# Self attention: the causal mask moves into stack rows and small column tiles, and the maxima's parts move from VectorE to GpSimd

## The reference

```python
# x: (16, 128, 256) float32; H = 16 heads of HD = 16
qkv = x @ Wqkv.T + bqkv
q, k, v = (to_heads(z) for z in jnp.split(qkv, 3, axis=-1))
q, k = _rope(q), _rope(k)
att = jnp.einsum('bhqd,bhkd->bhqk', q, k) * scale
att = jnp.where(jnp.tril(jnp.ones((t, t), dtype=bool)), att, -jnp.inf)
att = jax.nn.softmax(att, axis=-1)
y = jnp.einsum('bhqk,bhkd->bhqd', att, v)
y = y.transpose(0, 2, 1, 3).reshape(b, t, c) @ Wo.T + bo
...
x = _layernorm(x + y, axis=-1)
```

## Time and profile before

| | |
|---|---|
| median of 3 runs | 1186.73 us (1185.58 to 1187.6) |
| profiled execution | 1184.21 us |
| its span | 1182.4 us |
| granted clock, mean | 0.987 |
| PE busy over the span | 1113.7 us (94%) |
| DVE, ACT, Pool busy | 954.8, 669.1, 661.2 us |

### The profile page before, as it was taken

One profiled execution on the slowest core, in us unless ns is written; L12 is line 12 of the kernel. 1 busy time (PEld: TensorE's weight loads), 2 busy tenths in 40 slices (PEclk: granted clock), 3 DMA queues, 4 the chain that ended last, 5 costly groups with the idle time before them and its releaser, 6 DMA issues.

```text
span 1182.4 us, 30629 instructions
## 1 busy us (share of the span) xinstructions
PE 1113.7 (94%) x11732; PEld 920.0 (78%) x11732; DVE 954.8 (81%) x2219; ACT 669.1 (57%) x1703; POOL 661.2 (56%) x714
## 2 busy tenths in 40 slices
PE   6899999799999999888999999999999999999997
PEld 5667666566666766556899899999999899988887
DVE  6768877887878878867788888888888888868977
ACT  5466564577777777564555444444444444558663
POOL 4467564645555555264778554444544455737665
PEclk9899999999999999989999999999999999999999
DMA  5875544354444444302111000000000100101111
GB/s 160 212 185 132 128 125 112 97 138 123 126 121 131 119 126 126 104 21 89 61 66 55 1 1 1 1 1 1 1 1 1 37 2 1 37 19 36 37 37 36
DMA packets 107491, 83.05 MB, mean 70 GB/s; under 512 B 74172, under 2 KB 95804, under 8 KB 107346
## 3 DMA queue, kind: packets, MB, share of 16 engines
q1 hardware_dynamic: 107345, 81.10, 24.6%
HBM read 57.02 MB, written 23.07 MB: 68 GB/s over the span
## 4 chain that ended last, share of the span: by engine, by line
PE 56%; DVE 14%; issue 6%; POOL 4%; ACT 2%; SPq 1%; DMA 0%; POOLq 0%; DVEq 0%; ACTq 0%
PE bank L1632 5%; PE bank L1633 5%; PE bank L1634 5%; PE bank L1688 4%; PE bank L1661 4%; PE bank L663 4%; PE bank L641 3%; PE bank L560 3%; DVE B_nr L803 2%; PE bank L1648 2%; PE bank L1703 2%; PE bank L1701 2%; PE bank L1702 2%; PE bank L1649 2%; PE bank L1650 2%
## 5 line engine op out<-in xcount | busy, mean ns | idle before, releaser
L1936 POOL TENSOR_TENSOR C_QK<-C_t1b,C_t2b 128x512 f32<-128x512 f32 x128 | 168.8, 1319 | 227.2 <-DVE C_t2b L1775 226.6
L1772 DVE SCALAR_TENSOR_TENSOR C_t1b<-bank,C_bcol,C_tabs 64x512 f32<-64x512 f32 x256 | 192.0, 750 | 38.4 <-PE bank L1634 34.3
L803 DVE TENSOR_REDUCE B_nr<-bank 128x4 f32<-128x512 f32 x256 | 164.3, 684 | 24.3 <-PE bank L602 23.8
L1062 ACT ACTIVATE PT<-bank 128x512 f32<-128x512 f32 x224 | 130.1, 596 | 92.4 <-PE bank L641 90.8
L1632 PE MATMUL bank<-C_XTh,C_Wh 128*128 128x512 f32 x256 | 112.4, 439 | 5.7 <-DVE C_XTl L1621 1.9
L1868 ACT ACTIVATE C_P<-bank,C_nm 128x128 f32<-128x128 f32 x256 | 90.7, 367 | 34.2 <-DVE C_nm L1785 32.6
L1887 ACT ACTIVATE C_V<-bank 128x512 f32<-128x512 f32 x64 | 38.1, 597 | 124.1 <-PE bank L1650 122.5
L1633 PE MATMUL bank<-C_XTl,C_Wh 128*128 128x512 f32 x256 | 101.7, 397 | 0.0
L1634 PE MATMUL bank<-C_XTh,C_Wl 128*128 128x512 f32 x256 | 101.2, 395 | 0.0
L663 PE MATMUL bank<-PT,vpool 128*32 128x128 f32 x2048 | 97.1, 285 | 2.0 <-ACT OTf L1072 2.0
L1775 DVE SCALAR_TENSOR_TENSOR C_t2b<-bank,C_bcol,C_tabs 128x512 f32<-128x512 f32 x128 | 96.1, 751 | 1.8
(11 more groups left out here) (271 smaller groups left out, 3495.8 us busy)
## 6 DMA issues: line engine op xcount, KB each, us to landing
Adrq<-PB SPq DMA_DIRECT2D x16, 192.0 KB, 3.0
Adrk<-PB SPq DMA_DIRECT2D x16, 192.0 KB, 3.2
stk<-Adrq SPq DMA_DIRECT2D x16, 192.0 KB
stk<-Adrk SPq DMA_DIRECT2D x16, 192.0 KB
Bdrq<-PB SPq DMA_DIRECT2D x16, 192.0 KB, 3.0
stk<-Bdrq SPq DMA_DIRECT2D x32, 96.0 KB
Bdrk<-PB SPq DMA_DIRECT2D x16, 192.0 KB, 2.8
stk<-Bdrk SPq DMA_DIRECT2D x32, 96.0 KB
```

Of the source, the lines that this page charges most:

```text
L803: e.tensor_reduce(dst, bank[n % 2][:, :].rearrange("p (a b) -> p a b", a=4), AX.X, ALU.max, negate=True).then_inc(sem("m_dve"), 1)
L1062: e.activation(pt_of(n)[:, :], bank2(n)[:, :], ACT.Exp).then_inc(sem("e_act"), 1)
L1772: e.scalar_tensor_tensor(out=v4(t1b[kq][lo:lo + 64, :]), in0=v4(o[hi:hi + 64, :]), scalar=bc[hi:hi + 64, :], in1=tabsC[hi:hi + 64, 2 * kq ...
L1936: e.tensor_tensor(QK[v % 3][:, kq, :], t1b[kq][:, :], t2b[kq][:, :], ALU.add).then_inc(sem("rc_pool"), 1)
```

## The change

Three things:

1. The mask matmuls L595 and L632 of self attention go. Blocks of 32x32 above the diagonal get their large negative value through three more stack rows: rows 96 to 98 hold, for each of the first three blocks, which columns are that block (one side) and -1e30 where the block is later (the other side); the rows of maxima and ones move to 99 to 101. So pass1's matmuls have 99 rows instead of 96, pass2's 102 instead of 99. The four blocks on the diagonal are added by a new function `causal_blocks`, four column-tile matmuls of 128 columns for each unit and pass, behind the scores; they give the signals `s_pe` and `t_pe`. In a step below 64 PE's order becomes pass1, pass2, the blocks of pass1's unit, the blocks of pass2's unit, pv. The constant rows come in two DMAs instead of one.
2. `shift_parts` runs on Pool for both attentions, and first in Pool's step.
3. `turned` is four instead of two steps behind the parts for g < 16. ACT's copy and SP's DMA follow, to step 4g + 9.

```diff
@@ turned
-    turned = {shift_step(g) + (2 if g < 17 else 4 if g < 31 else 2): g for g in range(32)}
+    turned = {shift_step(g) + (4 if g < 16 else 2 if g < 17 else 4 if g < 31 else 2): g for g in range(32)}
@@ shift_parts, its callers
-    def shift_parts(e, q, g, name):
+    def shift_parts(e, q, g):
...
-        e.tensor_copy(nmb[L][:, :, :, 0, :], heads(nr)).then_inc(sem(name), 1)
-        q.wait_ge(name, 4 * b + 1)
+        e.tensor_copy(nmb[L][:, :, :, 0, :], heads(nr)).then_inc(sem("sh_pool"), 1)
+        q.wait_ge("sh_pool", 4 * g + 1)
...
@@ dve_ab
-            if s in shifts and shifts[s] < 16:
-                shift_parts(e, q, shifts[s], "sh_dve")
@@ pool_ab
+            if s in shifts:
+                shift_parts(e, q, shifts[s])
             if s in INITS:
                 init_values(*INITS[s])
...
-            if s in shifts and shifts[s] >= 16:
-                shift_parts(e, q, shifts[s], "sh_pool")
@@ pass1
-                if not L:
-                    q.wait_ge("consts", 1)
-                    q.wait_ge("ld_m", 48)
-                    e.matmul(scores, causalTb[:, :], identb[:, :].unsqueeze(1).to_broadcast([128, 4, 128]),
-                             start=True, stop=False, skip_group_check=True)
...
-                    rows, h = (slice(64 * t, 64 * t + 48), hs[j] % 16) if L else (slice(0, 96), hs[j])
+                    rows, h = (slice(64 * t, 64 * t + 48), hs[j] % 16) if L else (slice(0, 99), hs[j])
...
-                    if j == 3:
+                    if L and j == 3:
                         m.then_inc(sem("s_pe"), 1)
@@ pass2
-                if not L:
-                    q.wait_ge("consts", 1)
-                    e.matmul(bank2(n)[:, :].rearrange("p (a b) -> p a b", a=4), identb[:, :],
-                             causalTb[:, :].unsqueeze(1).to_broadcast([128, 4, 128]), start=True, stop=False, skip_group_check=True)
                 q.wait_ge(*shift_sem(b + 16 * L))
...
-                    rows, h = (slice(64 * t, 64 * t + 54), hs[j] % 16) if L else (slice(0, 99), hs[j])
+                    rows, h = (slice(64 * t, 64 * t + 54), hs[j] % 16) if L else (slice(0, 102), hs[j])
...
+        def causal_blocks(o, left, right, name):
+
+            for g in range(4):
+                own = slice(32 * g, 32 * g + 32)
+                m = e.matmul(o[own, :].rearrange("p (a b) -> p a b", a=4)[:, :, own], left[:, own],
+                             right[:, own].unsqueeze(1).to_broadcast([128, 4, 32]), start=False, stop=True, skip_group_check=True)
+            m.then_inc(sem(name), 1)
...
@@ pe_ab, the order in a step
                 if pass2_units(s):
                     pass2(pass2_units(s))
+            for n in pass1_units(s):
+                if n < NA:
+                    causal1(n)
+            for n in pass2_units(s):
+                if n < NA:
+                    causal2(n)
+            if s < NA:
                 for n in pv_units(s):
                     pv(n)
@@ sp_ab
-                row = 64 * hg + 48 if L else 96
+                row = 64 * hg + 48 if L else 99
...
-            load(STK[96:99, :, :].rearrange("p (i s) x -> p i s x", s=32)[:, :, 16:32, :],
-                 ot[0:3, :].rearrange("p (s x) -> p s x", x=128).unsqueeze(1).to_broadcast([3, 10, 16, 128]), "ones_A")
+            for half, rows in enumerate((3, 6)):
+                load(STK[96:96 + rows, :, :].rearrange("p (i s) x -> p i s x", s=32)[:, :, 16 * half:16 * half + 16, :],
+                     edge[3 * half:3 * half + rows, :].rearrange("p (s x) -> p s x", x=128).unsqueeze(1).to_broadcast([rows, 10, 16, 128]),
+                     "ones_A")
```

More of the change, by code:

```diff
@@ L132, in program @@
     tabs_ready = ("ld_A", 32), ("ld_B", 48)
-    ot = I["c_one"]
+    ot, edge = I["c_one"], I["c_edge"]
     NA, NN = 64, 320
@@ L462, in split @@
             e.tensor_tensor(pb[:, 2, :, :], y_[:, :, :], pb[:, 1, :, :], ALU.subtract).then_inc(sem(sp(kp, 0)[0]), 1)
-    def shift_parts(e, q, g, name):
-        L, b = divmod(g, 16)
+    def shift_parts(e, q, g):
+        L = g // 16
         q.wait_ge("m_dve", last_unit(g, NK[L] - 1) + 1)
@@ L471, in shift_parts @@
         heads = lambda a: a[:, :, :].rearrange("p k (g h) -> p g k h", h=16)
-        e.tensor_copy(nmb[L][:, :, :, 0, :], heads(nr)).then_inc(sem(name), 1)
-        q.wait_ge(name, 4 * b + 1)
[L474 to L478, removed]
+        e.tensor_copy(nmb[L][:, :, :, 0, :], heads(nr)).then_inc(sem("sh_pool"), 1)
+        q.wait_ge("sh_pool", 4 * g + 1)
+        e.tensor_tensor(heads(nb[L]), heads(nr), nmb[L][:, :, :, 0, :], ALU.subtract).then_inc(sem("sh_pool"), 1)
+        q.wait_ge("sh_pool", 4 * g + 2)
+        e.tensor_copy(nmb[L][:, :, :, 1, :], heads(nb[L])).then_inc(sem("sh_pool"), 1)
+        q.wait_ge("sh_pool", 4 * g + 3)
+        e.tensor_tensor(nmb[L][:, :, :, 2, :], heads(nb[L]), nmb[L][:, :, :, 1, :], ALU.subtract).then_inc(sem("sh_pool"), 1)
     def pe_ab(e, steps):
@@ L585, in pass1 @@
                     if not L:
-                        q.wait_ge("ones_A", 16)
+                        q.wait_ge("ones_A", 32)
                 if n % U[L] == 0 or (L and n % 8 == 0):
@@ L600, in pass1 @@
                     i3 = b % len(QS[L])
-                    rows, h = (slice(64 * t, 64 * t + 48), hs[j] % 16) if L else (slice(0, 96), hs[j])
+                    rows, h = (slice(64 * t, 64 * t + 48), hs[j] % 16) if L else (slice(0, 99), hs[j])
+                    alone = bool(kd) if L else j == 0
                     m = e.matmul(bank[n % 2][:, j * 128:j * 128 + 128], QS[L][i3][rows, h, :], (AS if kd else KS[L])[i3][rows, h, :],
-                                 start=bool(kd), stop=bool(kd) or j == 3, skip_group_check=not kd)
-                    if j == 3:
+                                 start=alone, stop=bool(kd) or bool(L and j == 3), skip_group_check=not kd)
+                    if L and j == 3:
                         m.then_inc(sem("s_pe"), 1)
@@ L608, in shift @@
             L = g // 16
-            q.wait_ge(*(("sh_pool", 4 * g - 60) if L else ("sh_dve", 4 * g + 4)))
+            q.wait_ge("sh_pool", 4 * g + 4)
             q.wait_ge("consts", 1)
@@ L638, in pass2, with causal1, causal2 @@
                     i3 = b % len(QS[L])
-                    rows, h = (slice(64 * t, 64 * t + 54), hs[j] % 16) if L else (slice(0, 99), hs[j])
+                    rows, h = (slice(64 * t, 64 * t + 54), hs[j] % 16) if L else (slice(0, 102), hs[j])
                     alone = bool(L) and (adds_mask(n) or not is_masked(n))
                     m = e.matmul(bank2(n)[:, j * 128:j * 128 + 128], (AS if kd else KS[L])[i3][rows, h, :], QS[L][i3][rows, h, :],
-                                 start=alone, stop=alone or j == 3, skip_group_check=not alone)
-                    if j == 3:
+                                 start=alone or not (L or j), stop=alone or bool(L and j == 3), skip_group_check=not alone)
+                    if L and j == 3:
                         m.then_inc(sem("t_pe"), 1)
+        def causal_blocks(o, left, right, name):
[4 more added lines that the diff above has]
+            m.then_inc(sem(name), 1)
+        def causal1(n):
+            q.wait_ge("consts", 1)
+            q.wait_ge("ld_m", 48)
+            causal_blocks(bank[n % 2], causalTb, identb, "s_pe")
+        def causal2(n):
+            causal_blocks(bank2(n), identb, causalTb, "t_pe")
         def pv(n):
@@ L800, in maxima @@
             if n % U[L] == 0 and b >= 2:
-                q.wait_ge("sh_pool" if L else "sh_dve", 4 * b - 4)
+                q.wait_ge("sh_pool", 4 * (b + 16 * L) - 4)
             q.wait_ge("s_pe", n + 1)
@@ L2430, in tables @@
     c["c_one"][3:6] = 0
+    block = np.arange(2048) % 128 // 32
+    r = np.arange(3)[:, None]
+    c["c_edge"] = np.concatenate([block == r, np.where(block > r, f(-1e30), f(0)), np.ones((3, 2048))]).astype(f).astype(bf)
     c["c_pick"] = np.repeat(np.eye(32, dtype=f), 3, axis=0).astype(bf)
```

## The result

The changed kernel is slower: 1203.38 us (median of 4 runs, 1198.78 to 1205.31) against 1186.15 for the kernel before, a ratio of 1.0154 (95% interval 1.0131 to 1.0177). The forecast was 1188.3 with a range to 1197. It was the fastest of the four runs; between the medians lie 17.2 us.

The account below looks back on a forecast made before the run. PE was taken to pace self attention (109.86 of 114.00 us busy). On 1184.21, 8.0 − 12.0 − 1.5 = −5.5 at step 54, then + 6.6 − 0.4 + 0.9 = +1.6; from the median 1186.73, 1188.3 us, range 1176 to 1197.

Parts of the forecast that it names:

- +8.0 early: PE ahead of group 0's pass2: DMA behind 12 stack loads, +9.1, −1.9 swallowed, +0.8 low clock; range 7 to 9.
- −13.5 in the middle: Steps 14 to 53: 12.0 us from 0.30 saved in each of 40 PE steps, plus 1.5 from DVE's relief.
- +7.1 late: Groups 12 to 14: DMA behind series of 12 loads, +6.6; old wait gone at step 72, −0.4; low clock, +0.9.
- The second load of constants ... I take nothing.: SP's queue ahead of all its steps: one more issue, 0 to 0.9 us, taken as nothing.
- What leaves a step of PE's moves all later steps forward.: Self attention's full stretch: PE, in order and 96% busy, passes on each step's saving of 0.30 us (0.21 to 0.33).
- the later maxima: DVE's maxima start some 0.3 us later in a step, but are wanted only two steps on: nothing.
- DVE's relief: Parts moved to Pool relieve DVE, whose maxima and copies partly cause PE's 4.1 us idle: 0 to 3, taken 1.5.
- the late queue doesn't hold PE: Rival, groups 12 to 14: SP's DMA comes early enough that PE has no late wait; 1178 us, chance 0.23.
- the early wait is absorbed: Rival, group 0: other PE work that waits behind fills its wait later; gain 7 more, 1181 us, chance 0.05.
- Pool becomes the pace: Rival, self attention: Pool's waits stay beside the added parts, half of the 12.0 is lost; 1195 us, chance 0.17.
- The blocks don't run beside each other: Rival, PE's column tiles: two blocks cost 0.44 a step, no saving is left; about 1200 us, chance 0.03.
- the forecast's 3.7 a group: Pool's parts by the skill's rule: twice DVE's 1.85, 44 us in the stage, time 1204; given no chance.

Follow-up runs that it names:

- turn2_edge: The change with the turn at two steps and the constant rows of nine of ten stack slots loaded before the wait for the weights; 1182.54 us, ratio 0.9976.
- pool_only: The kernel before with only `shift_parts` moved from DVE to first in Pool's step, full mask matmuls, turn at two steps; 1181.17 us, ratio 0.9990.
- late2: The change with the turn at two steps for groups 12, 13 and 14 alone; 1192.71 us, ratio 1.0093 to the kernel before.
- early2: The change with the turn at two steps for group 0 alone; 1195.13 us, ratio 1.0096 to the kernel before.
- pool_cut: turn2_edge with Pool's bias addition to X cut from 256 to 2 columns; 1179.44 us, ratio 0.9963 to the kernel before.

## Why the prediction was wrong

The forecast's sum was +8.0 early, −13.5 in the middle (12.0 and 1.5) and +7.1 late, +1.6 in all. Measured on the same cuts (step 17, step 54, end): +11.6, −8.0, +10.9, so +14.6. The mechanism that it named as deciding, the DMA behind SP's series at group 0 and at groups 12 to 14, is the one that the runs show. Four terms failed, all to the same side; the first three miss by 2.3, 1.3 and 5.5 us, the fourth by 3.8, together the 13.0 between forecast and span.

- **"The second load of constants ... I take nothing."** It was priced as one issue of SP, 0 to 0.9 us. Both loads of constants are issued in 0.63 us, so the issue is not what cost: transfers behind them landed later (the last section has the rows), step 0 is 2.3 us late, and turn2_edge gives that back. The rows cited (issues of other loads) did not price a transfer at all.
- **Early wait, +8.0.** The wait is 9.32 us where 9.1 was forecast; the DMA went out at 59.14, 2.7 later than the 56.44 it was to take, and PE was 2.3 late too. Beside 2.3 from the start, 9.3 arose between steps 0 and 17, of which 1.3 is more than forecast. PE's clock, for which the forecast had 0.8 (four steps, a number that no row gave), is part of that: between 60 and 70 us the granted clock was 0.61, where it had been 0.83, and L633 behind the wait takes 0.61 instead of 0.39, the level of L632 at 60.54 in the earlier trace rows.
- **"What leaves a step of PE's moves all later steps forward."** This is the term that failed most, by 5.5 us. The size of a step's saving was right (0.30 forecast, 0.32 in the timeline, 9.8 to 10.0 of PE's busy time in 36 steps); what failed is that it moves through. PE, 96% busy, had 4% of gaps only as long as its own work filled them. When the work shrank, the waits for other engines' copies showed up: PE's idle grew from 3.1 us to 8.8 in the change, and to 6.7 in turn2_edge. This is the reading that fits the runs; the later maxima, which the forecast put at nothing and for which PE waits 2.3 us in this stretch of the change, are a part that no run prices. DVE's relief is real, 3.0 us alone (pool_only), more than the 1.5 taken.
- **Late, +7.1.** Groups 12 and 14 came behind the series as forecast. From the series to the end the loss is 14.6 − 4.7 = 9.9 us, where 7.8 + 0.9 − 0.4 = 8.3 was forecast. The larger error is the start of the series: forecast 1.2 us ahead of PE's step, it came 1.0 behind it (+4.7 against +3.6). With two buffers it comes 0.6 ahead of that step (+2.4 against +3.0), so 1.6 of these 2.2 us are Pool's wait for the turn, which the forecast had left out. For the 0.9 of low clock no row gave the length.

That last wait was to be read in the code: `shift_parts` waits for `sh_pe`, and the change brings the turn it waits for into the same step. The forecast listed SP's queue as the only one that the step is moved past and said of Pool's parts that they would use up its wait ahead of L462. They did that (that wait is gone from Pool's list in the middle), and then Pool stood for PE instead, 30.8 us in all.

Of the rivals, "the late queue doesn't hold PE" is refuted by late2, and "the early wait is absorbed" by early2, each worth some 7 us by the ratios; of the 6.9 us that early2 wins by step 17 the middle takes up 2.0. "Pool becomes the pace" is refuted as it was put (pool_cut), though the loss it expected in the middle, half of the saving, is what happened, by another way. "The blocks don't run beside each other" is refuted by the timeline: 0.05 to 0.07 us for a block of four.

DVE's busy time fell by 22.5 us, not by the 30 of its parts. Of the rest, 4.3 us lie in three other operations that took longer with as many instructions: the rope's product tt<-ab,vpool (before and in the change),

```profile
L425 DVE TENSOR_TENSOR tt<-ab,vpool 128x512 f32<-128x512 f32 x13 | 9.3, 715 | 4.1 <-ACT ab L974 4.1
L425 DVE TENSOR_TENSOR tt<-ab,vpool 128x512 f32<-128x512 f32 x13 | 11.4, 879 | 4.3 <-ACT ab L987 4.3
```

stk<-stk (2.8 to 4.0) and rr<-rr,B_tg (8.6 to 9.6). Why they did, no run shows. The cost of the parts was right: on Pool the four operations on A_nmb take 17.67 us for 64 (us, then PE, PEld and Pool busy),

```profile
31.00:205.00 174.00, 3.79 (x16) 1.63 (x16) 17.67 (x64) 0.88 0.60 147
```

1.1 each group, as from the earlier trace rows, where DVE took 1.85. The rule of the Trainium skill's page "GPSIMD Engine Reference", section "4.1 Engine selection", that GpSimd is about two times slower in operations with two inputs, does not show in these on 128x16. Two of the four have two inputs: their medians are 240 and 218 ns on Pool, and were 413 and 175 on DVE. The other two are copies with one input, so the forecast's 3.7 a group took the rule further than it goes.

What stays open: which chain among PE, DVE, ACT and Pool holds the 6.7 us of idle that turn2_edge still has in the middle, and how much of that idle the new order on PE makes; and how much of the late loss is the lower clock behind the waits; no run separates them.

## What to carry to other kernels

Before a step is moved along a pipeline, list for each queue what is issued between the old and the new place, and for each buffer who must have read it by then: here the DMA fell behind 12 loads, and a single buffer made Pool wait for PE. A saving on the busiest engine counts in full only until another limit takes over; here 2.7 and 4.1 us of 10 came through. Before counting it in full, list the waits for other engines that the removed work may have covered. Where an engine runs behind another, the place of a small operation in its step can be worth more than its length: here 9.5 us for parts of 1.1 a group.

## What the runs showed of the hardware

Two loads of constants into few partitions (3 and 6, 120 and 240 KB) delayed the transfers behind them. Between 15 and 20 us the DMA engines were busy at a share of 0.33 and moved 52 GB/s in the change; before, with the 120 KB alone, 0.13 and 25; and in the change the fourth of SP's issues behind them took 4.3 us instead of 0.7. The two Adrq transfers took 6.6 us from issue to landing, where they had taken 2.6. The Trainium skill's page "DMA: Bandwidth & Descriptors", section "Rules for kernel authors", says that an outermost dimension smaller than 16 confines a DMA to at most that many engines. The low share is in line with it, and no run here changes the shape to prove it. The stretch before and in the change, then Adrq before and in the change:

```profile
15.00:20.00 5.00, 3.34 (x26) 2.93 (x24) 4.87 (x9) 2.48 (x5) 0.00 (x0) 1.00 0.13 25
15.00:20.00 5.00, 3.50 (x28) 3.05 (x26) 4.87 (x9) 2.65 (x5) 0.00 (x0) 1.00 0.33 52
...
Adrq<-PB SPq DMA_DIRECT2D x2, 192.0 KB, 2.6
Adrq<-PB SPq DMA_DIRECT2D x2, 192.0 KB, 6.6
```

The first of the four small operations was steadier on Pool than on DVE. In the change L472's CAST takes 188 to 672 ns, with a median of 196; on DVE it took 162 to 1894, with a median of 1006. What stretched it there, no run shows.
